# Graph attention on one core: keys and values in half-blocks, the next half's features between the present half's projections

## What is computed

```python
self_feat = concat(x, where(x.sum(-1) == 0, 0, cond)) @ W_self.T + b_self       # [B, N, F]
out = self_feat
for d in range(2):
    A = (adj if d == 0 else swap(adj))[:, :, :20]
    kv = self_feat[:, :20]                                # the first 20 nodes are keys
    q = self_feat @ Wq[d].T + bq[d];  k = kv @ Wk[d].T + bk[d]      # 16 heads of 32
    s = where(A.sum(-1) > 0, q.k / sqrt(32), NEG) + A @ w_bias + b_bias
    out += per head (softmax(s) @ kv) @ Wout[d].T + bout[d]
return x + relu(out)
```

## Time and profile before

| | |
|---|---|
| median of three runs | 1953.5 us (1951.45 to 1953.76) |
| the profiled execution's own time | 1954.26 us |
| its span, first to last instruction | 1952.5 us |
| mean granted TensorE clock | 0.993 |
| PE busy | 1914.4 us, 98% of the span |
| PE weight loads busy | 1669.7 us, 86% |
| DVE, POOL, ACT busy | 68%, 43%, 29% |
| first row-sum matmul of keys and values | 79.10 us |
| its last projection matmul | 405.21 us |
| first matmul of the main loop | 408.71 us |

### The profile page before, as it was taken

The page is one execution under the profiler, slowest core; times in us unless marked ns, Lnnn a source line. Parts: engine busy times, 40 slices in busy tenths (PEclk is TensorE's granted clock), DMA queues, the critical chain, the costliest instruction groups (busy, mean ns, idle before and its releaser), DMA issues.

```text
span 1952.5 us, 34072 instructions
## 1 busy us (share of the span) xinstructions
PE 1914.4 (98%) x10888; PEld 1669.7 (86%) x10888; DVE 1332.9 (68%) x1898; ACT 571.3 (29%) x1150; POOL 842.4 (43%) x723
## 2 busy tenths in 40 slices
PE   5899999999999999999999999999999999999999
PEld 3799999988888888888888888888888888888887
DVE  6624223267777777777777777777777777777776
ACT  1231322313232333333333332333223332332231
POOL 1422131134444444444444444444444444544443
PEclk9899999999999999999999999999999999999999
DMA  8423333273444444444444444444444444444421
GB/s 169 90 71 69 93 81 88 72 164 86 118 119 119 118 119 121 125 123 124 126 123 120 120 119 118 118 118 119 122 121 123 121 122 121 121 123 120 124 97 61
DMA packets 240765, 220.89 MB, mean 113 GB/s; under 512 B 57808, under 2 KB 195536, under 8 KB 236624
## 3 DMA queue, kind: packets, MB, share of 16 engines
q1 hardware_dynamic: 236256, 220.28, 42.7%
q10 hardware_dynamic: 4464, 0.02, 0.1%
HBM read 165.44 MB, written 54.79 MB: 113 GB/s over the span
## 4 chain that ended last, share of the span: by engine, by line
PE 77%; DVE 1%; DMA 1%; issue 0%; POOL 0%; ACT 0%; ACTq 0%; SPq 0%; DVEq 0%
PE bank L1306 35%; PE bank L1254 18%; PE bank L1242 12%; PE bank L1278 7%; PE bank L1267 4%; DMA adj<-in_mask_BxSxSx_ik 1%; PE bank L1227 0%; DVE nodes_t L83 0%; DVE qt_main L1065 0%; PE bank L1315 0%; DVE res L1052 0%; DVE sc L1029 0%; DVE res L1050 0%; DVE nodes_t L1001 0%; POOL rc L940 0%
## 5 line engine op out<-in xcount | busy, mean ns | idle before, releaser
L940 POOL TENSOR_TENSOR rc<-nzb,cqg 128x512 f32<-128x512 bf16 x256 | 265.1, 1041 | 412.1 <-DVE qt_main L1065 411.9
L1242 PEld LDWEIGHTS bank<-kbd,qt_main 128*128 128x128 f32 x2048 | 243.5, 192 | 19.5 <-DVE sc L1029 13.6
L1065 DVE SCALAR_TENSOR_TENSOR qt_main<-bank,bq_all,rc 128x512 f32<-128x512 f32 x256 | 189.4, 740 | 90.9 <-PE bank L1306 86.2
L918 POOL TENSOR_TENSOR sc<-sc,mx 128x640 f32<-128x640 f32 x128 | 163.4, 1277 | 199.0 <-DVE mx L1034 199.0
L1242 PE MATMUL bank<-kbd,qt_main 128*128 128x80 f32 x2048 | 247.4, 274 | 0.4 <-DVE sc L1029 0.2
L1152 ACT ACTIVATE wtt<-bank 128x384 f32<-128x384 f32 (+1 forms) x256 | 111.3, 436 | 381.0 <-PE bank L1267 380.9
L1040 DVE TENSOR_REDUCE sm<-sc 128x32 f32<-128x640 f32 x128 | 104.6, 818 | 162.8 <-ACT sc L1144 162.8
L1306 PE MATMUL bank<-nodes_h,wq_h 128*128 128x512 f32 x512 | 210.4, 411 | 0.0
L1306 PE MATMUL bank<-xh_odd,wq_h 128*128 128x512 f32 x512 | 210.4, 411 | 0.0
L1306 PE MATMUL bank<-xh_odd,wq_l 128*128 128x512 f32 x512 | 202.3, 395 | 0.0
L1306 PE MATMUL bank<-nodes_h,wq_l 128*128 128x512 f32 x512 | 202.2, 395 | 0.0
(11 more groups left out here) (120 smaller groups left out, 3915.2 us busy)
## 6 DMA issues: line engine op xcount, KB each, us to landing
rows<-in_x SPq DMA_DIRECT2D x128, 256.0 KB, 4.9
xk<-in_x SPq DMA_DIRECT2D x32, 1024.0 KB, 6.2
res<-c_dram SPq DMA_DIRECT2D x32, 1024.0 KB, 4.6
out<-res SPq DMA_DIRECT2D x128, 256.0 KB, 2.1
adj<-in_mask_BxSxSx_ik SPq DMA_DIRECT2D x32, 440.0 KB, 5.6
adj<-in_mask_BxSxSx_ik SPq DMA_DIRECT2D x128, 110.0 KB
k_dram<-kv_kst SPq DMA_DIRECT2D x64, 160.0 KB, 1.8
v_dram<-kv_vt SPq DMA_DIRECT2D x256, 40.0 KB
```

Source lines behind the costliest of these rows:

```text
L918: pool.tensor_tensor(s, s, mx[:, b % 2, :].unsqueeze(2).to_broadcast([P, DIRS * H, NG]), ALU.subtract).then_inc(s_shifted, 1)
L940: pool.tensor_tensor(rc[:, c % 2, :].rearrange("p (b n) -> p b n", b=G), nzb[:, par, :].rearrange("p (b n) -> p b n", b=G), cqg[:, par, c, ...
L1065: nc.vector.scalar_tensor_tensor(out=qt[:, c, :], in0=bank[c % 2][:], scalar=bq_all[:, c:c + 1], in1=rc[:, c % 2, :], op0=ALU.add, op1=ALU ...
L1242: mm = nc.tensor.matmul(dst, qt[:, c, b * N:b * N + N], kbd[:, c, :, b * NG:b * NG + NG], start=True, stop=True)
```

## The change

Keys and values now go in 8 half-blocks of 16 batches (320 columns, `HB`), n = 0 to 7, with parity `par` = n % 2. The parts of `rows`, `nodes_t`, `nodes_h` and `nodes_l` that held a block's two halves become the homes of even and odd half-blocks, and `kv_fh` and `kv_fl` have two homes too. The columns of a half-block are ordered so that partition q = 2b + h holds batch b and nodes 10h to 10h + 9; its x rows come in 8 DMAs of 16 partitions (`load_half_rows`) in place of 4 of 32 for a whole block. `prepare_weights` loads both first half-blocks, turns, casts and subtracts them in 8 pieces of 320 columns, all low parts on POOL. In `keys_and_values` PE makes the sums and features of half-block 0 by themselves; from then on each half-block's 16 projections have the row sums and the four feature groups of the next one between them. The number of matmuls of each kind is the same. The diff, cut to its core:

```diff
@@ load_block_rows / load_half_rows @@
-    xv = v["x"][bass.ds(k * KB, KB), 0:NG, :].rearrange("b m (i k) -> i b m k", k=P)
-    for i in range(NQ):
-        eng.dma_start(v["rows"][Q * i:Q * i + Q], xv[i]).then_inc(sem, 16)
+    dst = v["rows"][:, par * MH:par * MH + MH, :]
+    for i in range(NQ):
+        for mh in range(2):
+            src = v["x"][bass.ds(n * HB, HB), mh * MH:mh * MH + MH, i * P:i * P + P]
+            eng.dma_start(dst[Q * i + mh:Q * i + Q:2], src).then_inc(sem, 16)
@@ prepare_weights, vector @@
-            for j in range(C):
-                block_transpose(nc.vector, nodes_t[:, j, :], rows[:], j).then_inc(kv_turned, 1)
-            for j in range(3, C):
-                dve.wait_ge(kv_high, j + 1)
-                nc.vector.tensor_tensor(nodes_l[:, j, :], nodes_t[:, j, :], nodes_h[:, j, :].bitcast(F32),
-                                        ALU.subtract).then_inc(kv_low, 1)
+            for par in range(2):
+                dve.wait_ge(kv_loaded[par], 16 * HALF_LOADS)
+                for j in range(C):
+                    block_transpose(nc.vector, half(nodes_t, j, par), rows[:, par * MH:par * MH + MH, :],
+                                    j).then_inc(kv_turned, 1)
@@ keys_and_values, buffers and ring @@
+    SUM_SLOT = 2
+    FEAT_SLOT = (4, 6, 8, 10)
+    PROJ_SLOT = tuple(s for s in range(5 + 2 * NK) if s != SUM_SLOT and s not in FEAT_SLOT)
+    SLOTS = len(PROJ_SLOT) + len(FEAT_SLOT) + 1
+    def slot_bank(par, slot):
+        return bank[(SLOTS * par + slot) % RING][:, 0:HALF]
@@ sync @@
+            def one_half(blk, n, par, first, last, tail):
+                if not tail:
+                    sp.wait_ge(x_turned, C * (n + 1))
+                    load_half_rows(sp, v, n + 2, par, loaded[par])
...
+                for p in range(NK):
+                    sp.wait_ge(kv_out, 2 * NK * n + p + 1)
...
@@ vector @@
+            def one_half(blk, n, par, first, last, tail):
+                if not last:
+                    pick_condition(n + 1)
+                if not tail:
+                    turn_x(blk + 1, n + 2, par)
+                if not last:
+                    nonzero(n + 1, 1 - par)
+                    for j in range(C):
+                        features_out(n + 1, 1 - par, j)
...
@@ gpsimd @@
+            def one_half(blk, n, par, first, last, tail):
+                if not last:
+                    conditions(n + 1)
+                if not tail:
+                    x_lows(n + 2, par)
+                if not last:
+                    features_low(n + 1, 1 - par)
...
@@ scalar @@
+            def one_half(blk, n, par, first, last, tail):
+                for j in range(C):
+                    key_out(n, par, j)
+                    if not tail:
+                        x_cast(n + 2, par, j)
+                for j in range(C):
+                    key_out(n, par, C + j)
+                    if not last:
+                        feature_high(n + 1, 1 - par, j)
...
+                for m in range(NK):
+                    value_out(n, par, m)
@@ tensor @@
+            def one_half(blk, n, par, first, last, tail):
...
+                pe.wait_ge(f_low, C * (n + 1))
+                project(0)
+                project(1)
+                next_sums()
+                project(2)
+                next_features(0)
+                project(3)
+                next_features(1)
+                project(4)
+                next_features(2)
+                project(5)
+                next_features(3)
+                for p in range(6, 2 * NK):
+                    project(p)
+            sums(0, 0)
+            features(0, 0, 0)
+            features(0, 0, 1)
+            pe.wait_ge(nz_done, 1)
+            features(0, 0, 2)
+            pe.wait_ge(feat_out, 1)
+            features(0, 0, 3)
+            halves(pe, one_half)
```

More of the change, by code:

```diff
@@ L378, in _ @@
                                  bank[1][0:B, :].rearrange("b (j p) -> b j p", j=C), ACT.Copy).then_inc(crow_out, 1)
[L379 to L381 removed]
+            for par in range(2):
+                for j in range(C):
+                    act.wait_ge(kv_turned, C * par + j + 1)
+                    nc.scalar.activation(half(nodes_h, j, par), half(nodes_t, j, par), ACT.Copy).then_inc(kv_high, 1)
         @block.tensor
@@ L561, in _ @@
+                for m in range(NK):
+                    dve.wait_ge(kv_out, 2 * NK * n + NK + m + 1)
+                    if due(64 * (2 * n + m // 4)):
+                        dve.wait_ge(v_stored[m % 4], 64 * (2 * n + m // 4))
+                    nc.vector.transpose(vt[:, m % 4], vst[:, m % 2]).then_inc(v_turned, 1)
             pick_condition(0)
-            blocks(dve, KBLOCKS, one_block)
+            nonzero(0, 0)
+            for j in range(C):
+                features_out(0, 0, j)
+            halves(dve, one_half)
@@ L708, in _, with free @@
-            blocks(pe, KBLOCKS, one_block)
+            def free(n, par, slot, first, last):
+                a = SLOTS * par + slot
+                while True:
+                    a -= RING
+                    ago, s = divmod(a, SLOTS)
+                    m = n + (ago - par)
+                    projected = s in PROJ_SLOT
+                    if first and ago < par and projected:
+                        if a < -SLOTS:
+                            return
+                        continue
+                    if last and ago == par and not projected:
+                        continue
+                    break
+                if projected:
+                    pe.wait_ge(kv_out, 2 * NK * m + PROJ_SLOT.index(s) + 1)
+                elif s == SUM_SLOT:
+                    pe.wait_ge(nz_done, m + 2)
+                else:
+                    pe.wait_ge(feat_out, C * (m + 1) + FEAT_SLOT.index(s) + 1)
@@ new lines, in three, with sums @@
+            def three(dst, wh, wl, mh, ml):
+                for j in range(C):
+                    for k, (a, b) in enumerate(((wh, mh), (wh, ml), (wl, mh))):
+                        mm = nc.tensor.matmul(dst, a(j), b(j), start=(j == 0 and k == 0), stop=(j == C - 1 and k == 2))
+                return mm
+            def sums(n, par):
+                pe.wait_ge(x_low, C * n + C)
+                for j in range(C):
+                    for k, part in enumerate((xh, xl)):
+                        mm = nc.tensor.matmul(slot_bank(1 - par, SUM_SLOT), ones[:], x_cols(part, j, par),
+                                              start=(j == 0 and k == 0), stop=(j == C - 1 and k == 1))
+                mm.then_inc(pe_sum, 1)
@@ new lines, in one_half, with project, next_sums, next_features @@
+            def one_half(blk, n, par, first, last, tail):
+                def project(p):
+                    free(n, par, PROJ_SLOT[p], first, last)
+                    projection(n, par, p)
+                def next_sums():
+                    if not last:
+                        free(n, par, SUM_SLOT, first, last)
+                        sums(n + 1, 1 - par)
+                def next_features(jo):
+                    if not last:
+                        free(n, par, FEAT_SLOT[jo], first, last)
+                        features(n + 1, 1 - par, jo)
+                pe.wait_ge(f_low, C * (n + 1))
[12 more added lines that the diff above has]
+                    project(p)
```

349 lines of the change are left out of this document (150 added, 199 removed).

## The result

| | before | changed |
|---|---|---|
| median of five runs | 1953.21 us (1951.45 to 1953.76) | 1964.96 us (1960.94 to 1965.62) |
| the profiled execution's own time | 1954.26 | 1961.78 |
| first transpose at the end of the preparation | 69.25 us | 66.86 us |
| first row sum of keys and values | 79.10 us | 75.17 us |
| last projection | 405.21 us | 412.40 us |

A forecast was written before the change was run, and what follows sets the result against it. PE was taken to bound the kernel, busy 98%, the stage being its matmuls without pauses. Terms -2.0 + 2.5 + 0 + 0 + 0 = +0.5 us, laid on the median, gave 1954.0 us; range 1951 to 1962.

The forecast's parts named there:

- (a): End of the preparation, before the first row sum: PE starts 2.0 us earlier, bounds nothing to 2.1 us.
- (b): Before half-block 0's first projection: PE waits for all four feature chunks, 2.5 us lost once, bounds 2.3 to 3.0.
- (c): Start of keys and values: PE works longer at half clock, between -0.5 and +1.2 us, taken as 0.
- (d): After PE's stand in half-block 0: clock may fall, +1.5 to +3.1 us, chance about one in three, taken as 0.
- (e): Half-blocks 1 to 5, projection 4: wait for x loads nothing, 1.7 us in hand; 11.5 us at worst.
- rival 1: Half-block x loads land late, holding PE at the fifth key: slower, 1959 to 1966 us, chance 0.20.
- (f): Rest of the stage, its end and the main loop: matmul count, next chunks and other engines cost nothing.
- rival 2: Start of stage and first stand: clock falls and features suffer in it, +4.8 us, 1958.3 us, chance 0.06.
- Rivals 3 and 4: Keys-and-values features: one weight load hidden per change of kind, 1951.6 us, chance 0.06; loads several ahead, 1940 us, chance 0.04.

The follow-up runs named there:

- the filler: Changed kernel with x work moved behind the features on DVE, POOL and ACT, plus 16 unread row-sum matmuls in half-block 0's stand: 1953.30 us, ratio 0.9996.
- SP alone written out: Changed kernel with the keys-and-values loop written as straight code on SP only, the four other engines keeping the loop: 1955.92 us, ratio 1.0010.
- x behind the features: Changed kernel with the x work of half-block n + 2 moved behind the features of n + 1 on DVE, POOL and ACT: 1954.47 us, ratio 1.0011.

## Why the prediction was wrong

- **(a) End of the preparation**, -2.0 predicted: 8.31 for 9.85, so -1.54. Right in kind. DVE's small operations end at 74.30 us, POOL's eight pieces at 74.82, so POOL decides; they took 6.64 us, 0.83 each where I had 0.77, and began 1.32 us behind the first transpose.
- **(b) The stand**, +2.5 predicted: 2.71 for 0.23, +2.48. Right. (The 3.75 us named there as the work that hid the way is the length of the way itself, 105.61 to 109.35 us; what hid it were 36 matmuls of the first four projections, 5.3 us. The sum does not use the number.)
- **(c) The lower clock at the start**, 0 predicted between -0.5 and +1.2. By the starts it cost 2.0 us before, 0.4 in the first profile of the changed kernel and 1.4 in the second, so the term is -1.6 or -0.6, both below my lower bound. My premise failed that the clock comes back at the same time. PE stood 6.0 us ahead of the stage before, and the lower clock ended at 83.62; it stood 2.9 and 4.5 us in the two profiles, and the lower clock ended at 80.06 and 81.00.
- **(d) The stand brings the clock down**, taken as 0 with a chance of a third. It did, in all eight profiles that kept the stand and in none of the three that filled it. It lasted 3.4 us in six and cost 1.4 to 1.5 us by the starts (1.3 by the filler), and 6.8 us in two, the second profile of the changed kernel and that with SP alone written out, for 2.8 and 2.9. My bounds were 1.5 to 3.1. This went the other way from what I took, but by itself it would have stayed within the forecast. The fall in the long pause, 1.7 to 1.9 us more, was priced nowhere.
- **(e) The loads of x.** This is the step that failed: a wait taken as nothing, with 1.7 us in hand, that measured 6.5 to 6.7. It failed in two inputs, both about SP. The count to 13.8 us was exact. The landing, which I had singled out as the unknown and had bounded from 1.8 to 7.2, was 2.3 to 2.4, 0.9 better than I took. What I had taken as known was wrong: "SP gets there 3.24 us after" and "issues every 0.55 us" were read at one boundary, the first, which SP passes from straight code. The trace of before had two more. PE begins block 3 at 324.29, and SP's loads there are at 330.83, 6.54 us behind; PE begins block 2 at 243.22, and SP's loads there are at 250.88:

```profile
243.22 0.32 PE L677 MATMUL bank<-nodes_h,ones 128*128 128x320 f32 x1
```

```profile
249.41 0.75 SPq L495 DMA_DIRECT2D v_dram<-kv_vt  x2
250.88 0.90 SPq L70 DMA_DIRECT2D rows<-in_x  x2
```

  That is 7.66 us behind the boundary, with the value stores still going over 6 us into the new block. With 7.66 for 3.24 and my own landing of 3.2 the sum would have read 7.66 + 3.85 + 3.2 + 1.8 = 16.5 against 13.8, a wait of 2.7 us in each half-block that it held for, and in two or more of them that is rival 1. The second input is the issue distance of 0.55, which came from loads of another shape; an issue of the new shape took 0.58 to 0.66 us for 0.37, 0.64 apart in straight code, about 0.8 in the loop. In half-blocks 3 and 5 both were needed: SP came 1.8 us later than I took and needed 2.0 more for its eight issues, less 0.9 for the landing: 12.1 + 2.9 = 15.0, and either alone would have stayed within the 1.7 in hand. In half-block 4 it was 5.3 + 1.6 - 0.9 = 6.0, so 18.1.
- **(f) The rest** cost nothing, as said: nothing else makes PE wait, and from the last projection to the main loop it is 3.50 us in both. That DVE, ACT and POOL are busy for less than a third in these windows does not hold for POOL in the first, 10.04 of 22.00 us.
- **The rivals.** Rival 1 came, with its size (1959 to 1966, here with the clock's falls in it) and its sign (PE waits for ACT's `kv_kst` at the fifth key), but through SP's arrival and not through the landing by which I had weighed it, at 0.20. Of rival 2 the clock's half came too. Rivals 3 and 4 did not: at full clock the stage still adds up to 324.0 us, with features at 0.234 us, so no weight load was hidden at a change of kind.

In one line: predicted -2.0 + 2.5 + 0 + 0 + 0; found, at the last projection, -1.5 + 2.5 + 6.5 to 6.7 for the pauses and +2.0 to +4.4 for the clock and what is spread over the stage, less the 1.8 to 2.4 by which the preparation's end began sooner, which is not the change's.

## What to carry to other kernels

When a step is to wait for a queue, read when that queue gets there at every boundary of the old trace, in straight code and in the loop, and not at the first one; the issuing engine can be late where the transfers are fast. Do not put work that needs a fresh load ahead of a read that frees a bank: behind the features the same loads landed 6 us later than forecast (16.5 for 10.3) and cost nothing. And a single stand of PE costs more than its length, since the clock can fall behind it; filled with useful matmuls, a stand of 2.5 us gave back 4.0 (329.64 to 325.65 us, x behind the features in both).

## What the runs showed of the hardware

- The same loop branch on SP's queue took 0.33 us with 286 and 300 instructions in the loop's second pass, and 2.53 to 2.73 us in the eight kernels with 324. It was on the critical path in half-block 4 because eight loads stood right behind it. Why it takes so long is open: no row shows what SP does in the gap.
- In keys and values a load of 80 KB into 16 partitions took SP 0.58 to 0.66 us to issue in the changed kernel; of the eight loads of 320 KB into 32 partitions that the kernel before issues in its loop, seven took 0.35 to 0.37 and one 0.65. Smaller loads did not issue faster: those of 160 KB took 0.59 to 0.66 each. They landed in 2.8 to 3.7 us, the 80 KB ones of the loop in 2.3 to 2.4.
- A stand of PE of 2.3 us was followed by half clock for 3.4 or 6.8 us in all eight profiles that kept it; 16 unread matmuls in its place avoided that, and so did useful ones. In the changed kernel the pauses of 1.2 us in half-blocks 3 and 5 were not followed by a fall. A longer stand is not always followed by one: between the last projection and the main loop PE waits for 3.2 us or more in every version, and in three of the thirteen profiles, that of the changed kernel and those with the filler and with SP alone written out, the clock stayed at 2.4 GHz.
